# Three groups of instructions change their place in the order of a cross-attention phase of a two-layer decoder

## The reference, cut to what matters

```python
xn = layernorm(ctx, ln_x_g, ln_x_b)              # 32 x 361 x 192
ln = layernorm(layernorm(x), ln_l_g, ln_l_b)     # 32 x 100 x 256
q  = ln @ Wq.T
kv = concat([xn @ Wkv.T, ln @ Wlkv.T], axis=1)   # keys and values
qn = rmsnorm(q, qn_g) * 64 ** -0.5               # by head
kn = rmsnorm(k, kn_g)
attn = softmax(where(mask, qn @ kn.T, -max))
x = x + (attn @ v) @ Wo.T + bo
```

## Time and profile before

| | |
|---|---|
| time, median of 3 executions | 3773.59 us (3772.64 to 3778.21) |
| the profiled execution | 3778.21 us, of which the span of the profile is 3776.4 us |
| TensorE busy | 3528.7 us, 93% |
| weight loads | 2431.2 us, 64% |
| VectorE, ScalarE, GpSimd busy | 51%, 43%, 41% |
| instructions | 71408 |

### The profile page before, as it was taken

One profiled execution on the slowest core, in us unless ns is written; L12 is line 12 of the kernel. 1 busy time (PEld: TensorE's weight loads), 2 busy tenths in 40 slices (PEclk: granted clock), 3 DMA queues, 4 the chain that ended last, 5 costly groups with the idle time before them and its releaser, 6 DMA issues. The chain is left out here.

```text
span 3776.4 us, 71408 instructions
## 1 busy us (share of the span) xinstructions
PE 3528.7 (93%) x25692; PEld 2431.2 (64%) x25693; DVE 1920.0 (51%) x6166; ACT 1631.8 (43%) x3507; POOL 1563.3 (41%) x2142
## 2 busy tenths in 40 slices
PE   8997899998999778999799999999999989999998
PEld 5664455555777564444466666666666658899986
DVE  4664666664777654664454555544555447211113
ACT  4663455554666306777244444444444431111111
POOL 1001334433677414553355555555555547000025
PEclk9999999999999789999999999999999989999998
DMA  9401211100000153000100000000000001799962
GB/s 281 168 0 26 51 38 38 38 13 12 10 18 20 49 163 75 19 18 10 41 7 7 7 7 13 7 7 7 13 7 7 1 7 56 263 326 324 328 217 81
DMA packets 111418, 262.50 MB, mean 70 GB/s; under 512 B 24003, under 2 KB 70240, under 8 KB 95840
## 3 DMA queue, kind: packets, MB, share of 16 engines
q1 hardware_dynamic: 90208, 224.70, 18.5%
q0 software_dynamic: 16384, 26.29, 2.5%
q10 hardware_dynamic: 4608, 8.39, 0.6%
HBM read 196.61 MB, written 62.65 MB: 69 GB/s over the span
## 5 line engine op out<-in xcount | busy, mean ns | idle before, releaser
L2390 POOL TENSOR_SCALAR wide_probs<-wide_probs,wide_inverse 100x361 f32<-100x361 f32 x512 | 606.1, 1196 | 0.1
L2585 ACT ACTIVATE wide_probs<-wide_probs,wide_least 100x361 f32<-100x361 f32 x512 | 300.9, 589 | 618.0 <-DVE wide_least L2658 618.0
L2658 DVE CUSTOM_DVE_ANT_0 wide_probs<-banks,wide_bias 100x361 f32<-100x361 f32 x512 | 251.7, 529 | 218.9 <-issue 218.9
L2388 POOL TENSOR_TENSOR wide_hold_pool<-eps 100x1 f32<-100x1 f32 x256 | 50.6, 198 | 573.1 <-DVE wide_inverse L2664 573.0
L2446 PE MATMUL banks<-w_wide_v,wide_c 64*120 64x512 f32 (+1 forms) x1152 | 263.5, 589 | 2.5 <-DVE wide_v L2644 1.8
L2070 ACT ACTIVATE rot_h<-banks,w_rot_b 128x800 f32<-128x800 f32 x256 | 223.3, 923 | 86.9 <-PE banks L1944 83.3
L2440 PE MATMUL banks<-wide_c,w_wide_k 64*128 64x361 f32 x1536 | 256.0, 464 | 3.0 <-DVE wide_kT L2641 2.3
L2482 PEld LDWEIGHTS banks<-ident,wide_probs 100*120 100x120 f32 (+1 forms) x1536 | 158.3, 172 | 149.0 <-issue 118.3
L2468 PE MATMUL banks<-wide_kT,wide_qT 64*100 64x361 f32 x1024 | 220.9, 508 | 7.9 <-issue 7.9
L3089 ACT ACTIVATE tiles_hT<-banks 128x512 f32<-128x512 f32 x114 | 68.1, 597 | 348.3 <-PE banks L3005 348.3
L3005 PEld LDWEIGHTS banks<-tiles_xT,tiles_w 128*128 128x128 f32 x1824 | 214.1, 193 | 4.5 <-issue 1.6
(11 more groups left out here) (461 smaller groups left out, 7655.7 us busy)
## 6 DMA issues: line engine op xcount, KB each, us to landing
tiles_w<-in_moe_w SPq DMA_DIRECT2D x114, 1024.0 KB, 5.1
slots<-zeros SPq DMA_DIRECT2D x58, 512.0 KB, 5.7
cross_c<-in_ctxT SPq DMA_DIRECT2D x32, 270.8 KB, 4.4
wide_c<-in_ctxT SPq DMA_DIRECT2D x32, 270.8 KB, 4.0
mix_kT<-slots SPq DMA_DIRECT2D x32, 256.0 KB, 4.3
slots<-mix_kT ACTq DMA_DIRECT2D x32, 256.0 KB, 4.0
tiles_rows<-slots SPq DMA_DIRECT2D x57, 128.0 KB, 4.7
slots<-tiles_out SPq DMA_DIRECT2D x57, 128.0 KB, 4.9
```

Of the source, the lines that this page charges most:

```text
L2390: last = nc.gpsimd.tensor_scalar(t.probs[:, i % RING, j, :], t.probs[:, i % RING, j, :], t.inverse[:, i % RING, j:j + 1], None, ALU.mult)
L2585: last = nc.scalar.activation(t.probs[:, i % RING, j, :], t.probs[:, i % RING, j, :], ACT.Exp, bias=t.least[:, i % RING, j:j + 1], scale=-1.0,
L2658: last = nc.vector.tensor_tensor_reduce(t.probs[:, i % RING, j, :], scores(j), t.bias[:, :], -1.0, LARGEST, ALU.add, ALU.min, t.least[:, i ...
```

## The change

Only the order of calls within run() is changed, on three engines: on TensorE make_kv(after, 1) goes ahead of turn_probs(here, 0), turn_probs(here, 2) ahead of project(before, 1), and by_v(here, 1) ahead of turn_rows(third); on ScalarE weigh(here, 3) and keep_probs(here, 2) go ahead of keep_kT(after, 0), and keep_kT(after, 1) behind keep_rows(third); on VectorE norm_k(after, 1, 1) goes ahead of add(before, 1) and rows_apply(third). Waits, tiles, loads and the instructions themselves are the same.

```diff
@@ TensorE, run() @@
                 score(here, 1)
+                if after:
+                    make_kv(after, 1)
                 turn_probs(here, 0)
-                if after:
-                    make_kv(after, 1)
                 if before:
                     by_v(before, 3)
@@
                 score(here, 3)
+                turn_probs(here, 2)
                 pe.wait_ge(rep[0], here.n)
                 if before:
                     project(before, 1)
                 if after:
                     turn_k(after, 0)
-                turn_probs(here, 2)
+                by_v(here, 1)
                 if third:
                     if before:
                         pe.wait_ge(added[1], before.n)
                     turn_rows(third)
-                by_v(here, 1)
                 if after:
                     turn_k(after, 1)
@@ ScalarE, run() @@
                 if after:
                     widen_mask(after, 0)
+                weigh(here, 3)
+                keep_probs(here, 2)
                 if after:
                     keep_kT(after, 0)
-                weigh(here, 3)
-                if after:
-                    keep_kT(after, 1)
-                keep_probs(here, 2)
                 if third:
                     keep_rows(third)
                 if after:
+                    keep_kT(after, 1)
                     widen_mask(after, 1)
@@ VectorE, run() @@
                     norm_k(after, 1, 0)
                 mask(here, 3)
+                if after:
+                    norm_k(after, 1, 1)
                 if before:
                     add(before, 1)
                 if third:
                     rows_apply(third)
-                if after:
-                    norm_k(after, 1, 1)
                 keep_heads(here, 1)
```

More of the change, by code:

```diff
@@ L1397, in run @@
                 score(here, 1)
-                turn_probs(here, 0)
                 if after:
                     make_kv(after, 1)
+                turn_probs(here, 0)
                 if before:
```

## The result

Five executions of each kernel gave a median of 3800.65 us (3797.54 to 3806.0) after the change and 3778.21 us (3772.64 to 3783.88) before: a ratio of 1.0062, 95% interval 1.0046 to 1.008. The change costs 22 us, where the forecast was 6, and 3800.65 lies above the range.

What follows compares the result with a forecast made beforehand. TensorE's order, and when it may start its waiting items, was taken as the bound. Steady runs +3.8, run 0 +0.76 and run 14 +1.52 made +6.1, say 6.0, on 3773.6: 3779.6 us, range 3770 to 3788.

Steps and rivals of the forecast that it cites:

- the two waits: On TensorE in a steady run: make_q starts 0.76 us late for cross_kv, turn_rows 0.68 us late for cross_y.
- Part A: First half of a run: make_kv(after, 1) ahead of turn_probs(here, 0) lets make_q start 0.55 us earlier.
- the tie: At make_q, VectorE's keep_kv allowed a gain of 0.55 us and TensorE being free 0.49; 0.55 was taken.
- Part B: Second half of a run, moves on three engines: turn_k(after, 1) starts at 612.04 instead of 611.20, 0.84 us lost.
- The chain from the shift to turn_k(1): From VectorE's shift through ScalarE's weigh, keep_probs and cross_kT copy to TensorE: 3.35 us.
- The rule of the Trainium skill on shared ports: norm_k would wait for GpSimd's q_root, making the sum about 1.3 us more; the prediction didn't apply it.
- The sum: Whole phase: 13 steady runs give +3.8, run 0 +0.76, run 14 +1.52, together +6.1 us.
- rival 3: TensorE's clock falls after the new 1.1 us wait, about 1.7 us a run, 27 in all: 3807 us; chance 0.03.

Runs made afterwards that it cites:

- a_only: Kernel before with only make_kv(after, 1) moved ahead of turn_probs(here, 0): 3770.88 us, ratio 0.9982.
- act_only: Kernel before with only ScalarE's three moves, TensorE and VectorE as before: 3806.22 us, ratio 1.0078.
- act_fill: Kernel before with ScalarE's three moves and five transposes added in TensorE's wait for cross_kT: 3797.19 us, ratio 1.0054.
- pe_only: Kernel before with only TensorE's moves, ScalarE and VectorE in the order of before: 3762.43 us, ratio 0.9955.
- fill: Changed kernel with nine transposes added in TensorE's wait for cross_kT: 3788.1 us, ratio 1.0021 of before.
- run 0: Not a follow-up kernel: the first of the phase's 16 calls of run(), without add and project; forecast +0.76 us.
- run 13: Not a follow-up kernel: the call of run() that ends the 13 steady ones (1 to 13), each forecast at +0.29 us.
- run 14: Not a follow-up kernel: the call of run() after the steady ones, without turn_rows; forecast +1.52 us.
- fill4: Changed kernel with four transposes added in TensorE's wait for cross_kT: 3782.22 us, ratio 1.0017 of before.
- fill_y: Changed kernel with five transposes ahead of turn_rows(third), the wait for cross_kT left whole: 3784.43 us, ratio 1.0018 of before.
- split: Changed kernel with by_v(here, 1) put back behind turn_rows(third): 3790.41 us, ratio 1.0028 of before.
- after_again: The changed kernel itself, run and traced a second time: 3804.97 us, ratio 1.0071 of before.

## Why the prediction was wrong

**What bounds the phase** was right: TensorE's order, and on it the two waits. The wait of make_q went and the one for cross_kT came, as forecast; the one for cross_y only shrank from 0.68 to 0.58 us, where less than 0.3 had been forecast.

**Part A** was a little too large. a_only gives 0.43 us a run (6.5 / 15). Of the two bounds in the tie, 0.55 and 0.49, the second was nearer: in the rows above by_v at 633.55 + 0.84 releases make_q at 634.39, so TensorE itself is the bound, and 634.39 - 629.89 = 4.50 is what 2.76 + 0.90 + 0.84 had given. The 0.13 from ScalarE's copy to make_kv(1) was 0.15 (628.67 + 1.07 = 629.74 to 629.89).

**Part B, the schedule,** was right in its main term. The chain from the shift to turn_k(1) had been 3.35 us; it is 617.05 - 613.71 = 3.34 (VectorE's shift at 613.55, 0.16 long). The wait for cross_kT is 1.14, as forecast. turn_rows waited 0.58 and not under 0.3, mostly since project took 0.86 us of TensorE (612.10 to 612.96) and not the 1.20 that I had allowed. The period without a fall of the clock is 32.50, 0.1 above the 32.4 forecast.

**The rule of the Trainium skill on shared ports** ("SBUF — State Buffer", "Who interferes with whom") was set against norm_k in its new place. In the changed kernel q_root ran on GpSimd from 613.23 for 1.78 us, and norm_k started at 613.63, inside it, and took 0.68 as ever. It wasn't held back; q_root took 1.78 instead of 1.65. That is so in every trace: the median of q_root is 1.78 us in the kernels that have norm_k in the new place and 1.65 in those that don't (before, a_only, act_only, act_fill, pe_only), and the median of norm_k 0.68 to 0.69 before and after. So the overlap cost GpSimd 0.13 us and VectorE nothing. turn_rows started 1.64 us after the shift's end, where the sum without the rule had 1.76 and the sum with it would have had 2.94.

**The sum** of the schedule, +6.1, is also what fill measures in the phase, 504.5 - 498.4 = 6.1, but that the two agree to the tenth is luck. From turn_k(1) of run 0 to that of run 13 it is 417.44 us before and 422.21 in fill: +4.8 for the 13 steady runs, where I had 3.8; 0.37 a run instead of 0.29, for the most part because part A gave 0.43. Run 14 adds 1.6 (forecast 1.5), and run 0, counted from the score at 398.35 (397.60 in fill), 0.76 as forecast. That is 7.1. Against it stands the start of the phase: before, make_lkv of run 0 fell to half speed behind its wait of 2.79 us (5.34 us), and in fill it didn't, though its wait was 2.52, which makes about 1.6 us less:

```profile
394.02 3.65 PE L1299 MATMUL banks<-w_cross_lkv,cross_lT 128*100 128x512 f32 x8 [2.52 <-DVE cross_kv L1615]
```

The last run adds 0.5 in fill, where the clock fell once more (0.57 from 880 to 884 us). fill4 and fill_y, with the same schedule, come to 5.4 and 7.1. All traces but those of before and a_only have the quicker start, so every other phase set against 498.4 us has some 1.6 us in its favour that no reordering brought.

**The step that failed is rival 3, the clock,** which the sum put at nothing. I gave it 0.03 on two readings. One was that only an idle stretch of 2.79 us had lowered the clock and that waits of 0.76 and 0.68 had not the earlier trace rows. The other, unspoken, was that waits count one by one. The new wait fell right behind an old one, with only the short turn_rows between them, and the pair lowered the clock in most runs. The price was 1.1 to 1.3 us for a fall in a steady run, not 1.7, and 12 runs paid it, not 16: 15.6 us in the first trace, where 27 stood. That fill, fill4 and fill_y each give it back, though they add work and leave the schedule as it is, is what shows the clock to be the cause; act_only and act_fill show the same on the kernel before with ScalarE's moves.
The Trainium skill tells of such a case: "TensorE: Matmul & The Clock Gate", section "A second HAM failure mode: psum-queue depth-cycling", describes a kernel whose short idle times between groups of matmuls, and not one long gap, made the clock go down and up again. The trace agrees: no single wait was over 1.14 us in the steady runs, and turn_k(1) went from 0.99 to 1.77 us.

**What stays open.** Which pattern of waits lowers the clock. The sum of the idle time doesn't say (split, 1.71 us, held; act_only, 0.68 + 0.75, fell), nor does the longest wait (1.14 in fill_y and 1.42 in split held), nor that there are two (fill4, 0.58 + 0.69, held). The work around differs too: act_only has turn_k and turn_probs ahead of its first wait, split has project and turn_k. So does the length of a run, 34.15 us in act_only and 32.50 in split; since runs 6 and 7 of the changed kernel have the same waits and only one fell, the moment at which the waits come must count as well, and split and act_only could differ by that. Neither was tried. Nor is it shown where some 3 us of fill's whole time (9.5 against 6.1 in the phase) and 7 of after_again's (26.4 against 19.5) lie; whole times of one kernel scatter by 10 us and more.
The forecast of range and chances failed with the rival: a rival that had the place right deserved far more than 0.03, and the range should have reached to it. The two lengths set against each other, 0.76 and 2.79, leave the new wait of 1.1 between them. The trace of before even had a row that spoke for a single wait of 1.1 being harmless, and it would have misled all the same, since here one long wait wasn't what mattered:

```profile
404.64 1.59 PE L1306 MATMUL banks<-cross_lT,w_cross_q 128*128 128x200 f32 x8 [1.61 <-DVE cross_kv L1612]
```

That is make_q of run 0, at full speed behind a wait of 1.61 us.

## What to carry to other kernels

When a reordering gives TensorE a new wait, add to its price what the granted clock may lose, above all where the wait lands next to another: here a schedule 6 to 7 us longer brought 16 us of clock. Whether it is the clock can be tried in one run: give TensorE useless work in the wait that nothing else hangs on, and see if the kernel gets faster. A copy that frees a bank for TensorE goes first on ScalarE when it is ready, ahead of work that nobody waits for yet; undoing that one part turned a loss of 0.6% into a gain of 0.4%.

## What the runs showed of the hardware that I had not expected

Two waits of 0.58 and 1.14 us with 0.5 us of transposes between them were followed by a half-speed stretch of 3.2 us on TensorE in most runs, while 1.14 us alone, or 1.42 and 0.29 with 1.3 us of work between, were not (one steady window in the latter). But 0.68 and 0.75 us with the same 1.3 us of work between were, in each of runs 1 to 14 of act_only. The same two waits lowered the clock in one run and not in the next, in the changed kernel with every fifth steady run spared, and it could fall more than a microsecond after TensorE was back at work. VectorE's norm_k, running while GpSimd made its power (q_root), made that 0.13 us longer (1.78 instead of 1.65) and took no longer itself (0.68). Nine transposes that nobody reads made the kernel 0.4% faster (3788.1 against 3804.97 us on the same chip). And an unchanged last stage of the program took 94 us in one profiled execution and 113 to 117 in the other eleven, which made the slower kernel's profiled execution the faster one of the two. The granted clock in it was 0.96 there and 0.88 in that of before; why isn't shown.
